# Both first weight groups on tiles 0 to 3 before the later tiles, and x tiles 5 to 7 requested after the first weight part

## The reference, cut to what matters

```python
xn = layernorm(x)                                   # x: (4, 4096, 1024)
# s: decaying outer-product state, read by q
k, v, q = xn @ Wk, xn @ Wv, xn @ Wq                 # 64 columns each
g = sigmoid(xn @ Wg + bg)
S = decay * S + outer(k * g, v * g);  s = (q @ S) @ Wo + bo      # token by token
# f: feed-forward of 3072 hidden units, integer weights times 1/127
h = silu(xn @ w_gate.T / 127) * (xn @ w_up.T / 127)
f = h @ w_down.T / 127
out = x + s * silu(f)
```

## Time and profile before

| | before |
|---|---|
| median of three runs | 512.41 us (510.85, 512.41, 512.44) |
| the profiled execution | 510.7 us, span of its slowest core 509.1 us |
| spans of the eight cores | 507.0 to 509.1 us |
| TensorE | 489.0 us busy, 96% of the span |
| VectorE, ScalarE, GpSimd | 360.2, 188.1, 128.9 us busy |
| granted TensorE clock, mean of a core | 0.998 to 1.000 |
| busy share of the 16 DMA engines, 0 to 41.2 us | 0.97 |

### The profile page before, as it was taken

The page is one execution under the profiler, slowest core; times in us unless marked ns, Lnnn a source line. Parts: engine busy times, 40 slices in busy tenths (PEclk is TensorE's granted clock), DMA queues, the critical chain, the costliest instruction groups (busy, mean ns, idle before and its releaser), DMA issues.

```text
span 509.1 us, 8811 instructions; the slowest of 8 cores (507.0 to 509.1 us)
## 1 busy us (share of the span) xinstructions
PE 489.0 (96%) x2722; PEld 238.2 (47%) x2722; DVE 360.2 (71%) x683; ACT 188.1 (37%) x296; POOL 128.9 (25%) x193
## 2 busy tenths in 40 slices
PE   4799999999999999999999999999999999999996
PEld 2455455555554444444554444444444444444442
DVE  4767677676668889977665767677776678966534
ACT  2534545554443331246512443343333342112111
POOL 3636322422326201636352421211111000000000
PEclk9999999999999999999999999999999999999999
DMA  8999999999999941297789997656666500053352
GB/s 231 223 138 155 156 146 154 138 158 153 150 127 206 153 134 39 95 272 203 219 207 175 164 178 100 88 85 83 84 84 88 77 2 1 21 146 88 100 143 82
DMA packets 37452, 66.77 MB, mean 131 GB/s; under 512 B 3295, under 2 KB 12639, under 8 KB 37408
## 3 DMA queue, kind: packets, MB, share of 16 engines
q0 software_dynamic: 18672, 36.19, 50.4%
q1 hardware_dynamic: 14928, 26.22, 17.3%
q10 hardware_dynamic: 3808, 3.81, 2.6%
HBM read 89.28 MB, written 8.39 MB: 192 GB/s over the span
## 4 chain that ended last, share of the span: by engine, by line
PE 78%; DVE 7%; DMA 5%; issue 4%; POOL 3%; ACT 2%; DVEq 0%; ACTq 0%; SPq 0%; POOLq 0%
PE bank L475 52%; PE bank L531 19%; DMA gu<-wgu 3%; DMA xs<-xtm 1%; PE bank L655 1%; ACT xnt_all L1147 1%; PE bank L543 1%; PE bank L467 1%; PE bank L637 1%; DVE bst L863 1%; PE bank L619 1%; DVE bst L864 1%; PE bank L457 1%; POOL rs L1269 1%; POOL t L1280 1%
## 5 line engine op out<-in xcount | busy, mean ns | idle before, releaser
L475 PE MATMUL bank<-xs,S_w 128*128 128x512 f16 x552 | 139.2, 379 | 0.0
L475 PE MATMUL bank<-xnT,gu 128*128 128x512 f16 x368 | 94.4, 379 | 0.9 <-DVE S_w L727 0.6
L475 PEld LDWEIGHTS bank<-xs,S_w 128*128 128x128 f16 x552 | 52.5, 98 | 59.8 <-issue 0.2
L1232 POOL DMA_DIRECT2D gu<-wgu x48 | 26.3, 547 | 174.3 <-PE bank L475 163.1
L1062 DVE TENSOR_TENSOR bank<-bank,m 128x512 f32<-128x512 f32 x46 | 32.1, 700 | 45.6 <-PE bank L475 45.6
L475 PEld LDWEIGHTS bank<-xnT,gu 128*128 128x128 f16 x368 | 34.9, 98 | 40.9 <-issue 1.5
L745 DVE SCALAR_TENSOR_TENSOR hT<-bank,sg_all 128x512 f16<-128x512 f32 x69 | 46.6, 687 | 5.3 <-PE bank L475 4.5
L1070 DVE TENSOR_TENSOR m<-bank,m 128x512 f32<-128x512 f32 x46 | 31.7, 691 | 23.7 <-PE bank L475 22.8
L475 PE MATMUL bank<-xs,gu 128*128 128x512 f16 x184 | 47.2, 379 | 0.7 <-DVE m L1070 0.7
L475 PE MATMUL bank<-xnT,S_w 128*128 128x512 f16 x184 | 47.2, 379 | 0.0
L1188 ACT ACTIVATE bank<-bank 128x512 f32<-128x512 f32 x46 | 26.8, 582 | 48.4 <-PE bank L475 48.4
(11 more groups left out here) (161 smaller groups left out, 717.6 us busy)
## 6 DMA issues: line engine op xcount, KB each, us to landing
gu<-wgu POOLq DMA_DIRECT2D x96, 256.0 KB, 7.2
xr<-xtm SPq DMA_DIRECT2D x16, 512.0 KB, 6.2
out<-xr SPq DMA_DIRECT2D x32, 256.0 KB, 2.3
wd<-wdt POOLq DMA_DIRECT2D x24, 256.0 KB, 9.8
xs<-xtm SPq DMA_DIRECT2D x8, 512.0 KB, 4.2
xr<-xpfm POOLq DMA_DIRECT2D x8, 512.0 KB, 10.0
hT<-gu SPq DMA_DIRECT2D x5, 512.0 KB, 6.7
wd<-xtm SPq DMA_DIRECT2D x4, 512.0 KB, 16.1
```

The lines of the kernel that those rows point to most:

```text
L475: mm = pe.matmul(out=out[:], lhsT=weight(d), rhs=moving(d), start=(start and d == 0), stop=(d == 3), skip_group_check=True)
L1232: g.dma_start(out=gu[idx % NGU][:, 0:1024], in_=wgu[idx % NHC][:, 0:1024]).then_inc(ld_gate[idx % NGU], 16)
```

## The change

The list is rewritten from the first weight loads to the fourth projection, and SP's loads of tiles 5 to 7 get a wait for the first weight part.

```diff
-              ("stats", 2), ("norm", 2), ("wa_load", 0), ("ev", 0), ("tr", 2), ("warm", 8), ("ev", 1),
-              ("stats", 3), ("norm", 3), ("gate_load", 1), ("tr", 3), ("warm", 4),
-              ("ev", 2), ("stats", 4), ("norm", 4), ("up_load", 1), ("ev", 3), ("decay_1", 0), ("gate_load", 2)]
+              ("warm", 6), ("stats", 1), ("norm", 1), ("gate_load", 1), ("tr", 1), ("warm", 3),
+              ("stats", 2), ("norm", 2), ("ev", 0), ("tr", 2), ("warm", 8), ("ev", 1),
+              ("stats", 3), ("norm", 3), ("up_load", 1), ("tr", 3), ("warm", 4),
+              ("ev", 2), ("stats", 4), ("norm", 4), ("wa_load", 0), ("ev", 3), ("decay_1", 0)]
...
+    order += [("gate", 0), ("plain", 0), ("up", 0), ("tr", 4), ("gate_load", 2), ("stats", 5), ("norm", 5),
+              ("gate", 1), ("plain", 1), ("h", 0), ("ev", 4), ("up_load", 2), ("tr", 5), ("stats", 6), ("norm", 6),
+              ("up", 1), ("ev", 5), ("gate_load", 3), ("kvg", 0), ("kvg", 1), ("tr", 6), ("h", 1),
+              ("kvg_ev", 0), ("stats", 7), ("norm", 7), ("up_load", 3), ("kvg_ev", 1), ("ev", 6),
+              ("kvg", 2), ("kvg", 3), ("tr", 7), ("ev", 7), ("kvg_ev", 2), ("kvg_ev", 3),
+              ("gate_load", 4), ("up_load", 4), ("px_load", 0)]
...
                 if stage == "x_load" and i < 12:
-                    if i >= 8:
+                    if i == 5:
+                        y.wait_ge(ld_gate[0], 16)
+                    elif i >= 8:
```

More of the change, by code:

```diff
@@ L88, in stage_order @@
     order += [("decay_0", 0), ("warm", 13), ("gate_load", 0), ("stats", 0), ("norm", 0), ("up_load", 0), ("tr", 0),
-              ("warm", 6), ("stats", 1), ("norm", 1), ("tr", 1), ("warm", 3),
-              ("stats", 2), ("norm", 2), ("wa_load", 0), ("ev", 0), ("tr", 2), ("warm", 8), ("ev", 1),
-              ("stats", 3), ("norm", 3), ("gate_load", 1), ("tr", 3), ("warm", 4),
-              ("ev", 2), ("stats", 4), ("norm", 4), ("up_load", 1), ("ev", 3), ("decay_1", 0), ("gate_load", 2)]
[L93 to L98, removed]
+              ("warm", 6), ("stats", 1), ("norm", 1), ("gate_load", 1), ("tr", 1), ("warm", 3),
[8 more added lines that the diff above has]
+              ("gate_load", 4), ("up_load", 4), ("px_load", 0)]
+    order += [("gate", 2), ("plain", 2), ("up", 2), ("TS_0", 1), ("h", 2), ("kvg", 4), ("kvg_ev", 4),
               ("px_load", 1)]
```

## The result

| | before | after |
|---|---|---|
| median | 512.42 us (510.85 to 512.76, 4 runs) | 520.04 us (519.50 to 520.58, 4 runs) |
| the profiled execution | 510.7 us | 519.75 us |
| span of its slowest core | 509.1 us | 518.2 us |
| granted TensorE clock, mean of a core | 0.998 to 1.000 | 0.987 to 0.994 |

The changed kernel is slower: ratio 1.016 with a 95% interval of 1.0139 to 1.0180. The forecast was 515.6 with a range of 512.9 to 518.0: the direction was right, the size was not. The medians in this document hold the executions in which one die ran longer at a lower clock, the ratios leave them out, so the two can differ a little. Core 4 is again the slowest, so its rows can be laid beside those of before.

What follows compares the result with a forecast made beforehand. TensorE, busy 96% of the span, was taken as the bound, with no later wait to absorb delays. Gate 2's 3.2 us delay added to 512.4 (509.1 span + 1.6 outside + 1.7 to the median) gave 515.6 us, range 512.9 to 518.0.

Steps and rivals of the forecast that it cites:

- the lower bound of tile 5's landing: Earliest landing of tile 5 on SP: 18.9, from gate 0 landing at 14.4 with turns of 2.2 us.
- the bound for `wa`: Ahead of the first projection: `wa` at most 1.3 us late, if engines idle while gate 0's landing passes through SP.
- The chain of tile 7: First projection to gate 2: evacuation, statistics, norm, transposes and copy take 7.5 us, so gate 2 starts 3.2 us later.
- SP's wait: Tile 5, held for gate 0's weights, lands at 21.8, tile 7 at 28.8; tile 5's transposes wait 1.7 us.
- x too late: Rival: gate 0 lands at 17.4, tile 5 at 23.8, tile 7 at 31.8; gate 2 5.1 us late, 517.5 us; chance 0.08.
- Up 1's and `wa`'s weights: Ahead of the first projection: no delay charged; `wa` lands near 28.0, 0.6 us ahead of need; up 1's landing not forecast.
- I charge nothing: No delay for gate 1's weights (bound 0.9 us) nor for `wa` (bound 1.3 us).
- The estimate that the prediction worked out from the Trainium skill: By a fixed 2.0 us plus bytes at 436 GB/s, `wa` would land 2.9 us after issue, near 22.5.
- The clock: Rival: the clock falls in thin work before gate 2; gate 2 and up 2 take 2.4 us more, 518.0; chance 0.10.
- The start: Gate 0 keeps its start at 19.06, as the chain to it and its loads are in the old order.
- Behind gate 2: First paired product 8.28 us after gate 2, at 44.4; up 3 lands at 39.7 to 41.6 and costs nothing.
- Not slower: Rival: tile 1 earlier, tile 5 by 20, `wa` by 26; gate 2 0.8 us late, 513.2 us; chance 0.22.

Runs made afterwards that it cites:

- e1: The changed kernel without SP's wait, new order kept: 518.53 us, ratio 1.0111 to the kernel before.
- e3: The changed kernel with statistics and norm of tile 7 and up 3's load listed ahead of the first projection: 516.71 us, ratio 1.0093 to before.
- e5: The changed kernel with up 1's load issued right behind gate 1's: 517.61 us, ratio 1.0113 to the kernel before.
- e9: e7 with `wa`'s load behind the statistics of tile 3 and tile 7's transposes ahead of the fourth projection: 513.43 us, ratio 1.0021 to before.
- e7: The changed kernel with the edits of e1, e5 and e3 together: 512.23 us, ratio 1.0019 to the kernel before.
- e6: The changed kernel with 17 unread matmuls in the waits between first projection and gate 2: 519.16 us, ratio 1.0128 to the kernel before.
- e11: The changed kernel with the edits of e5 and e6 together: 516.83 us, ratio 1.0086 to the kernel before.
- e2: The kernel before with SP's wait ahead of tile 5 alone: 516.84 us, ratio 1.0090 to the kernel before.
- e4: The changed kernel with 33 unread matmuls between stages from tile 5's transposes to gate 2: 522.25 us, ratio 1.0196 to the kernel before.

## Why the prediction was right in direction and wrong in size

The sum can be redone on core 4. A wait in brackets is 0.16 us shorter than the delay it makes, since a matmul's end is drawn that much late; the delays below include it.

| step | predicted | measured | difference |
|---|---|---|---|
| gate 0 starts | 19.06 | 19.87 | +0.8 |
| delay ahead of the transposes of tile 5 | 1.7 | 0.4 | -1.3 |
| delay for up 1's weights | 0 | 2.6 | +2.6 |
| delay for `wa` | 0 | 1.2 | +1.2 |
| first projection to gate 2 | 7.5 | 7.9 | +0.4 |
| gate 2 to the first paired product | 8.28 | 10.45 | +2.2 |
| later than before at the paired product | 3.2 | 9.06 | +5.9 |

In the mean over the cores the paired product is 8.0 us later than before, and it starts 9.7 us behind gate 2, 1.4 more than before. Some of the prediction's figures are off without effect: the lower bound of tile 5's landing is 19.0 with its own 0.1 us of hand-over, the bound for `wa` is 1.4 us late by its own terms (28.0 + 2.0 - 28.6), and the trace of before has a third wait of TensorE between gate 0 and gate 2, 0.22 us ahead of the third projection.

**The chain of tile 7: right.** The term that was said to decide is there, at 7.50 us on core 4 of e1 and 7.49 us on core 5 of after (31.03 to 38.52). On core 4 of after it is 7.90, as the clock had begun to fall: the transposes of tile 7 took 1.01 us, not 0.61. e3 confirms the cause by moving the statistics.

**SP's wait: right on core 4, not on all.** Gate 0 landed at 15.8 (issued at 8.09, 7.7 us on; 15.9 forecast), tiles 5 and 7 within 0.5 us of the forecast. The delay of tile 5 was 5.4 us where 5.8 had been split into a start-up of 2.3 and a turn of 3.5. The next two turns were 2.6 and 4.7 us (tile 6 landed at 23.9, where 25.3 was forecast), so equal turns did not hold even here. Nor did the landing on other cores: tile 5 landed between 19.4 and 26.7 us in the kernels with this wait. Core 0 of after, with tile 5 at 23.7 and tile 7 at 30.1, comes near the rival "x too late". A sum for one core hides that spread, and the slowest of eight cores sets the time.

**Up 1's and `wa`'s weights: the step that failed.** The prediction put both at nothing. "I charge nothing" was said of gate 1's weights, from their place in the queue, and again of `wa`, which was to land "near 28.0" by a count of bytes over full engines. Of the landing of up 1 it wrote no line at all. The engines were busy indeed, but POOL's queue was empty: gate 1 was in at 18.3, up 1 issued only at 16.92, its bytes not flowing before 22.0. Meanwhile SP's tiles had the engines. Then up 1 and `wa` shared them with tiles 6 and 7 and landed at 28.8 and 31.7. A count of bytes over all queues says when everything has landed; it doesn't say when one queue's part has. How much of up 1's lateness is the empty queue and how much the late issue is not separated: within after the two cores with hardly a gap had up 1 some 2 to 4 us earlier than the others (issued 0.6 to 1.6 us earlier), but in e1, without any gap, it was hardly earlier than in after. The bound of 1.3 us for `wa` took an idle engine as the only danger and missed an idle queue. The first projection was 3.3 us later than 28.6; e5 takes back 2.8 us of it in the mean by an earlier issue of one load. For `wa` an earlier issue did not help: in e9 it landed later than in e7.

The estimate that the prediction worked out from the Trainium skill ("DMA: Bandwidth & Descriptors", "Anatomy of one DMA — SWDGE (gpsimd) path"), `wa` some 2.9 us behind its issue, is refuted further: 11.3 us here, and up 3, a smaller load, took 6.8 us though the engines were nearly idle in the first 3 us behind its issue.

**The clock: named, and mispriced in its chance.** The rival stood in the text with 0.10 and 2.4 us; every core had a stage at the slow clock between 28 and 46 us, six of the eight gate 2 or up 2, and it cost 2.2 us behind gate 2 on core 4. The mark that it was to show by, rows at the slow level behind 30 us, is the one that the trace has. The evidence that was held against it (a single gap of 1.24 us that did no harm) was about a gap, whereas here TensorE did 3.6 us of small work in 7.5 us with three gaps of about 1 us. e6 and e11 fill just this stretch and gate 2 and up 2 take 1.89 us on all cores, which shows the cause. The rival priced gate 2 and up 2 alone; that up 1 was slow too on four cores came, on three of them, with the wait for its weights that the prediction had missed. The Trainium skill's rule in "TensorE: Matmul & The Clock Gate", "Part 1: The HAM clock gate", that the clock follows recent activity, agrees.

**The start: not foreseen, and not the change's.** The constants landed at 7.5 us on core 4 instead of 5.9, and gate 0 was 0.8 us later (0.5 in the mean over the cores, 19.15 to 19.63). No edit touches the constants' load. Kernels with the same code ahead of gate 0 as after had means of 19.22 (e6) to 20.13 (e3), so 0.5 us is no more than one launch differs from another.

**Behind gate 2: right.** S1 had up 3's weights at 43.3, later than the 39.7 to 41.6 forecast since POOL issued them at 36.47, not 33.2, and cost nothing, the later order absorbs nothing, and no later wait is new.

**The rivals on the other side.** "Not slower" needed `wa` by 26 and had 0.22. It fell with the same missing step, since the queue was late by 5.7 us against that.

## What to carry to other kernels

Follow each DMA queue by itself, from issue to issue: a load's place in the list of work sets when it is issued, and a queue that runs dry while the others keep the engines full loses its turn, though the total of bytes is the same (0.81 MB of SP's tiles and nothing of POOL's from 18.6 to 21.6 us). When work is moved ahead of a chain, ask what covered that chain until now; here the two stages that moved were its cover, and putting the chain's first step ahead (e3) took 0.67 of the 1.60% back, at least as much as either edit to the transfers (0.49 for e1, 0.47 for e5). Where TensorE is left with small stages between waits, price the slow clock for the stage behind them, and check it on all cores.

## What the runs showed of the hardware that was not expected

A load issued by POOL needs several us before its bytes flow, even on idle engines: POOL issued up 3 at 36.47 us and gate 4 and up 4 within the next 1.2 us, the DMA share from 36.5 to 39.5 was 0.05, and up 3 landed 6.8 us behind its issue. Up 1's bytes began no sooner than 5.1 us behind its issue at 16.92. An issue 4.0 us earlier (e5) landed up 1 7.5 us earlier in the mean. It is no rule: `wa`, issued 3.6 us earlier in e9 than in e7, landed 1.5 us later.

The granted clock fell though no idle time between the first projection and gate 2 was longer than 1.36 us (core 4 of after; on core 3 of e5 there is no longer one from 20 us on, and gate 2 took 3.57 us), and it came back within up 2 (gate 2 3.57 and up 2 2.42 us, then 1.89). Longer waits elsewhere did the same: 6.52 us in e2, 5.31 us in e4.

The landing of a load that had been held back varied by 7 us among cores and launches with the same loads in the same order (tile 5 in after, e3, e4 and e6: 19.4 to 26.7 us, 4.7 to 9.6 us behind its issue). In the kernel before, where it is requested with the rest, it landed at 16.8 to 19.8 us.
